# The last 512 tokens of a linear-attention layer as two groups of 256

## The reference

```python
xn = _ln(x, ln_w, ln_b)
q = xn @ Wq + bq
k = xn @ Wk + bk + (1.0 - src_mask) * -1000000.0
q = softmax(q.reshape(b, t, h, dh), axis=-1)
k = softmax(k.reshape(b, t, h, dh), axis=1)
v = ((xn @ Wv + bv) * src_mask).reshape(b, t, h, dh)
att = einsum('bnhd,bnhl->bhdl', k, v)
y = einsum('bnhd,bhdl->bnhl', q, att).reshape(b, t, d)
scale, shift = split(silu(emb) @ W_emb + b_emb, 2)
hh = _ln(y, ln2_w, ln2_b) * (1.0 + scale) + shift
return x + silu(hh) @ W_out + b_out
```

## Time and profile before

| what | value |
|---|---|
| median of 3 runs | 334.37 us (333.7 to 336.6) |
| the profiled execution, its own time | 336.49 us |
| its span, first to last instruction | 334.7 us |
| mean granted TensorE clock over the span | 0.985 of full speed |

### The profile page before, as it was taken

How to read it: one execution, slowest core, us unless ns; L and a number is a source line. 1 busy time by engine, 2 the same in 40 slices (tenths; PEclk the granted TensorE clock), 3 DMA queues, 4 the chain that set the end, 5 groups by cost and what they waited for, 6 DMA issues and landing times.

```text
span 334.7 us, 14404 instructions
## 1 busy us (share of the span) xinstructions
PE 315.3 (94%) x5644; PEld 269.0 (80%) x5644; DVE 277.3 (83%) x749; ACT 182.7 (55%) x360; POOL 198.3 (59%) x261
## 2 busy tenths in 40 slices
PE   3999999999999999999999999999999999998736
PEld 1478777988879898988888898989898888988625
DVE  3695888989898989989897979799898989886771
ACT  1327574566484755565574847565556648454240
POOL 2305137767766775767677667757676775747420
PEclk9999999999999999999999999999999999999896
DMA  7702010040404021030304040210304010101011
GB/s 238 256 0 66 20 47 4 2 129 2 127 5 118 7 66 59 11 115 0 125 0 125 0 125 0 71 55 25 101 0 125 0 63 0 66 4 63 4 66 63
DMA packets 19418, 19.68 MB, mean 59 GB/s; under 512 B 817, under 2 KB 18865, under 8 KB 19394
## 3 DMA queue, kind: packets, MB, share of 16 engines
q1 hardware_dynamic: 18144, 17.96, 17.2%
q10 hardware_dynamic: 1250, 1.39, 1.3%
HBM read 10.95 MB, written 8.39 MB: 58 GB/s over the span
## 4 chain that ended last, share of the span: by engine, by line
PE 87%; DVE 5%; POOL 3%; DMA 2%; issue 1%; ACT 1%; SPq 0%; POOLq 0%; DVEq 0%
PE bv L674 29%; PE bk L674 28%; PE by L674 13%; PE by L734 4%; PE by L745 4%; PE by L777 4%; PE by L724 4%; DMA q_t<-in_wv 2%; POOL y_s L350 1%; DVE ystat L647 1%; DVE y_s L640 1%; POOL yr L345 1%; DVE z_s L565 0%; DVE q_s L557 0%; DVE rq L636 0%
## 5 line engine op out<-in xcount | busy, mean ns | idle before, releaser
L408 ACT ACTIVATE k_t<-k_t 128x512 f32<-128x512 f32 x32 | 20.2, 632 | 55.9 <-DVE k_t L591 55.9
L243 POOL TENSOR_TENSOR h_lo<-h_s,h_hi 128x512 fp32r<-128x512 f32 x30 | 38.1, 1290 | 10.0 <-ACT h_hi L434 10.0
L239 POOL TENSOR_TENSOR z_s<-z_s,mod_shift 128x512 f32<-128x512 f32 x30 | 30.7, 1043 | 21.6 <-DVE z_s L565 21.6
L674 PE MATMUL bv<-w_o_hi,h_hi 128*128 128x256 f32 x128 | 35.1, 295 | 4.5 <-ACT h_hi L434 4.5
L358 POOL TENSOR_TENSOR x_all<-x_all,bo_all 128x1024 f32 (+1 forms) x16 | 38.3, 2396 | 0.0
L391 ACT ACTIVATE xt_hi<-by 128x512 fp32r<-128x512 f32 x32 | 17.5, 595 | 37.1 <-PE by L745 37.1
L587 DVE TENSOR_REDUCE kmax<-bk 128x8 f32<-128x512 f32 x32 | 22.0, 687 | 16.2 <-PE bk L674 16.2
L350 POOL TENSOR_SCALAR y_s<-y_s,yr 128x256 f32<-128x256 f32 x62 | 33.8, 558 | 2.6 <-POOL yr L347 2.2
L345 POOL TENSOR_TENSOR yr<-yr,neg_half 128x4 f32<-128x4 f32 x16 | 16.2, 1012 | 31.4 <-DVE yr L654 31.4
L674 PE MATMUL bv<-w_o_lo,h_hi 128*128 128x256 f32 x128 | 34.7, 292 | 0.0
L440 ACT ACTIVATE xhat<-x_all,xr 128x256 f32 (+1 forms) x64 | 33.1, 590 | 2.3 <-POOL xr L333 2.3
(11 more groups left out here) (106 smaller groups left out, 857.6 us busy)
## 6 DMA issues: line engine op xcount, KB each, us to landing
x_all<-in_x SPq DMA_DIRECT2D x16, 512.0 KB, 4.5
out<-x_all SPq DMA_DIRECT2D x15, 512.0 KB, 3.2
z_s<-in_w_emb ACTq DMA_DIRECT2D x1, 512.0 KB, 8.6
h_s<-in_w_emb ACTq DMA_DIRECT2D x1, 512.0 KB, 10.5
out<-x_all SPq DMA_DIRECT2D x2, 256.0 KB, 2.1
y_s<-in_wk SPq DMA_DIRECT2D x1, 256.0 KB, 3.3
q_t<-in_wq SPq DMA_DIRECT2D x1, 256.0 KB, 5.5
th<-in_cond_t ACTq DMA_DIRECT2D x1, 256.0 KB, 7.2
```

The costliest lines, as they stand in the source:

```text
L239: return eng.tensor_tensor(z, z, mod_shift[:, c, span(g, GB)].unsqueeze(2).broadcast_to([P, GB, SEQ]), ALU.add)
L243: return eng.tensor_tensor(h_lo[:, c, :], h_s[:, c, :], h_hi[:, c, :].bitcast(fp32), ALU.subtract)
L408: nc.scalar.activation(k_t[:, par, c, :], k_t[:, par, c, :], ACT.Exp).then_inc(kexp_d, 1)
L674: return nc.tensor.matmul(dst, lhsT, rhs, start=start, stop=stop)
```

## The change

The last 512 tokens become two groups of 256 tokens: 15 groups of four tiles and two of two, G = 17. There are 19 working turns where there were 18. The loop has five passes (turns 3 to 12), and turns 13 to 18 are unrolled. In groups 15 and 16 each operation over a group's tokens is half as wide, or there are half as many of them; the output product keeps its matmuls of 256 columns, 12 of them for such a group. Every semaphore count that was a multiple of the group number is now the sum of the tiles (`tile0`) or pairs of tiles (`pairs`) before the group. A group of two tiles has no qv tiles 2 and 3, so its turn goes from y to o at once. The first k of turn 16 waits for `ksub_d`, since no q tiles used its bank.

```diff
-    G = ROWS // GT
     T = GT // P
+    TILES = [4] * 15 + [2, 2]
+    G = len(TILES)
+    R = ROWS // GT
+    LOOP = 5
...
-            with eng.Fori(1, G // 2 - 1) as turn:
+            with eng.Fori(1, LOOP + 1) as turn:
                 body(2 * turn + 1, 1, True, True, True, True)
                 body(2 * turn + 2, 0, True, True, True, True)
-            for i in range(G - 1, G + 2):
+            for i in range(2 * LOOP + 3, G + 2):
                 at(i)
...
+        def tile0(g):
+
+            return sum(TILES[0:max(g, 0)]) if isinstance(g, int) else g * T
+
+        def pairs(g):
+
+            return tile0(g) // 2 if isinstance(g, int) else g * 2
+
+        def size(g):
+
+            return TILES[g] if isinstance(g, int) else T
...
+        def last_pair(g, e):
+
+            return pairs(g) + (min(e, size(g) // 2 - 1) if isinstance(g, int) else e) + 1
...
-                    for t in range(T) if not last_y(i) else (0, 1):
+                    for t in range(n // 2 if last_y(i) else n):
...
-                    for e in range(2):
-                        wait(act, ekt_d, 2 * g + e + 1)
+                    for e in range(size(g) // 2):
+                        wait(act, ekt_d, pairs(g) + e + 1)
...
-                    v_tile(i, par, 2)
-                    v_tile(i, par, 3)
+                    for t in range(2, size(i)):
+                        v_tile(i, par, t)
...
-                if F:
+                if F and size(i) > 2:
                     q_tiles(i, par, (2, 3))
...
-                        wait_apart(pe, qsub_d, 4 * i + c - 1)
+                        if not (isinstance(i, int) and i < 1):
+                            if size(i - 1) > 2:
+                                wait_apart(pe, qsub_d, tile0(i - 1) + c + 3)
+                            else:
+                                wait(pe, ksub_d, 2 * i + c - 1)
+                        n = size(i) * P
...
-                    qv_tile(i, 2)
-                    qv_tile(i, 3)
+                    for t in range(2, size(i)):
+                        qv_tile(i, t)
...
-                    for e in range(2):
-
-                        wait(pe, qsub_d, 4 * i + e + 1 if F else 4 * G)
+                    for e in range(size(g) // 2):
+
+                        wait(pe, qsub_d, tile0(i) + e + 1 if F else tile0(G))
```

More of the change, by code:

```diff
@@ L236, in shift, with h_low, cut, x_of @@
         def shift(eng, g, c):
-            z = z_s[:, c, :].rearrange("p (b s) -> p b s", s=SEQ)
-            return eng.tensor_tensor(z, z, mod_shift[:, c, span(g, GB)].unsqueeze(2).broadcast_to([P, GB, SEQ]),
+            n = size(g) * P
+            z = z_s[:, c, 0:n].rearrange("p (b s) -> p b s", s=SEQ)
+            return eng.tensor_tensor(z, z, mod_shift[:, c, batches(g)].unsqueeze(2).broadcast_to([P, n // SEQ, SEQ]),
                                      ALU.add)
[L242 to L253, removed]
+        def h_low(eng, g, c):
+            n = size(g) * P
+            return eng.tensor_tensor(h_lo[:, c, 0:n], h_s[:, c, 0:n], h_hi[:, c, 0:n].bitcast(fp32), ALU.subtract)
+        x_h = x.rearrange("(n p) d -> p n d", p=P)
+        o_h = out.rearrange("(n p) d -> p n d", p=P)
+        def tile0(g):
[4 more added lines that the diff above has]
+            return TILES[g] if isinstance(g, int) else T
+        def cut(first, n):
+            return slice(first, first + n) if isinstance(first, int) else bass.ds(first, n)
+        def x_of(g):
+            return x_all[:, cut(tile0(g), size(g)), :]
+        def x_tile(g, t):
+            return x_all[:, cut(tile0(g) + t, 1), :].rearrange("p n d -> p (n d)")
+        def batches(g):
+            return cut(tile0(g) * 2, size(g) * 2)
+        def last_pair(g, e):
+            return pairs(g) + (min(e, size(g) // 2 - 1) if isinstance(g, int) else e) + 1
         @block.sync
@@ L283, in _ @@
             steps(sp, body)
-            for e in range(2):
[L286 to L290, removed]
+            last = tile0(G - 1)
+            for e in range(size(G - 1) // 2):
+                sp.wait_ge(res_d, pairs(G - 1) + e + 1)
+                sp.dma_start(o_h[:, last + 2 * e:last + 2 * e + 2, :],
+                             x_all[:, last + 2 * e:last + 2 * e + 2, :]).then_inc(stored, 16)
+            sp.wait_ge(stored, 16 * (G - 1 + size(G - 1) // 2))
         @block.gpsimd
@@ L432, in body @@
                         wait(act, h_d, 2 * g + c + 1)
-                        wait(act, o_d, 2 * g)
-                        nc.scalar.activation(h_hi[:, c, :], h_s[:, c, :], ACT.Copy).then_inc(hhi_d, 1)
+                        wait(act, o_d, pairs(g))
+                        nc.scalar.activation(h_hi[:, c, 0:size(g) * P], h_s[:, c, 0:size(g) * P], ACT.Copy).then_inc(hhi_d, 1)
                 if N:
@@ L702, in qv_tile @@
                 if t < 2:
-                    wait(pe, qsub_d, 4 * i + t - 3)
-                    wait(pe, res_d, 2 * (i - 3) + t + 1)
+                    if not (isinstance(i, int) and i < 1):
+                        wait(pe, qsub_d, tile0(i - 1) + t + 1)
+                    if not (isinstance(i, int) and i < 3):
+                        wait(pe, res_d, last_pair(i - 3, t))
                 else:
@@ L719, in exp_k_transposed @@
                 wait(pe, kexp_d, 2 * g + 2)
-                for e in range(2):
-                    wait(pe, ys_d, 2 * (g - 1) + 2)
+                for e in range(size(g) // 2):
+                    wait(pe, ys_d, pairs(g))
                     for t in (2 * e, 2 * e + 1):
@@ L741, in body @@
                         if c == 0:
-                            wait(pe, xhat_d, 4 * i + 4)
-                        wait(pe, ys_d, 2 * (i - 2) + 2)
-                        for t in range(T):
+                            wait(pe, xhat_d, tile0(i + 1))
+                        if not (isinstance(i, int) and i < 2):
+                            wait(pe, ys_d, pairs(i - 1))
+                        for t in range(size(i)):
                             last = nc.tensor.transpose(bt[c][:, t * P:t * P + P], xhat[:, par, t, c * P:c * P + P],
@@ L782, in body @@
                     g = i - 1
[L783 removed]
+                    wait(pe, ek_d, pairs(g + 1))
                     wait(pe, zs_d, 2 * g)
[L785 to L786 removed]
+                    wait_apart(pe, v_d, tile0(g + 1))
+                    for b in range(2 * size(g)):
                         t, e = b // 2, b % 2
```

205 lines of the change are left out of this document (103 added, 102 removed).

## The result

The changed kernel takes 340.07 us (median of 4 runs, 338.24 to 340.90); before, beside it, 335.19. The ratio is 1.013, with a 95% interval of 1.0096 to 1.0165: slower by 1.3%, about 4.4 us. The forecast was 336.6 in a range of 333.4 to 339.2, with "within 1%" at 0.74 and "slower" at 0.20. It was wrong. The ratios compare only executions in the faster of two states and are not exactly the quotient of the two medians; where a change in us stands behind a ratio, it is worked out from the ratio.

What follows compares the result with a forecast made beforehand. TensorE bounds the full turns, a serial chain through all engines the last 30 us. Drain -12.2, earlier T -2.1, new turn +14.9, clock +1.6: +2.2 on the median 334.37 gives 336.6 us, range 333.4 to 339.2.

Steps and rivals of the forecast that it cites:

- Up to turn 15: nothing: Turns before 15: unrolling turns 13 and 14 costs 0, hidden by TensorE's work.
- plus and minus 0.8 us for pauses: Allowance for TensorE pauses like the known 0.79 us one: -0.8 to +0.8 us.
- Turn 15 and turn 16: Turn 15's T comes 2.1 us earlier; the new turn 16 adds 14.9 us between the two T.
- The wait for h_lo: In turns 15 and 16, o issues four matmuls, then waits for h_lo; 1.6 us in turn 15.
- T: Landmark: the moment at which the second qv tile of a turn is done.
- The drain: Serial chain behind the last T: shrinks from 37.0 to 24.8 us.
- clock term: Loss from TensorE's low clock on the path: 1.6 us, ends 0 and 4.5 us.
- Clock, one stretch of 1.6 us in o of turn 16: In o of turn 16, behind waits, one stretch at 1.2 GHz adds 1.6 us, all on the path.
- upper widths listed: Upper uncertainties: narrow ScalarE pieces +0.4, kv +0.3, pauses +0.8, clock +2.9 us.
- Rival 2: Turns 15 to 17: TensorE becomes short bursts at 1.2 GHz; +5.1, 339.5 us; chance 0.18.
- Rival 3: Waits of turns 15 and 16 don't come, GpSimd and VectorE being ahead; -2.5, 331.9 us; chance 0.12.
- Rival 1: Clock keeps its level over o of turn 16; +0.6, 335.0 us; chance 0.25.

Runs made afterwards that it cites:

- u1: Kernel before with 16 full groups, loop one pass shorter, so turns 13 and 14 are unrolled: 338.0 us, ratio 1.0062 to the kernel before.
- second series: The changed kernel run once more as it is, beside other runs on one chip: 342.9 us, ratio 1.0195 to the kernel before.
- r1: Changed kernel with its loop kept at six passes, so turns 13 and 14 stay in it: 338.19 us, ratio 1.0073 to the kernel before.
- rf1: Six-pass version of the changed kernel plus five unused TensorE matmuls in the h_lo waits of turns 15 and 16: 337.53 us, 1.0059 to the kernel before.

## Why the prediction was wrong

- **"Up to turn 15: nothing", unrolling at 0, plus and minus 0.8 us for pauses.** This step failed. It looked at turn 15, which was unrolled and had no gap, and took it for all unrolled turns. The one pause it knew (0.79 us) was already of this kind, as the packet 2.4 us ahead of it shows; the forecast gave it a few tenths more if a cover were gone. Unrolling two turns alone costs 2.1 us (u1), in the changed kernel's own trace 3.2 us with the low clock behind the pause, in its second series still more. Without this term the size holds: six passes gave +2.5 us, forecast +2.2.
- **Turn 15 and turn 16.** The wait for h_lo was right: 1.33 us, forecast 1.6. But o of turn 15 then ran at the low clock and ended 7.6 us behind T in r1, forecast 6.0. Taking the start of y for T, the two T lie 15.7 us apart in r1 (294.16 to 309.82), forecast 14.9. With the clock held up by fillers, yT waited 0.82 us for the normalized y and came 9.2 us behind T, much as forecast (1.1 and 9.0).
- **The drain.** Behind the second T r1 has 25.6 us (309.82 to 335.4), forecast 24.8 without the clock term. From the start of turn 15 to the end of the span r1 took 50.6 us (284.80 to 335.4), the kernel before 48.2. The forecast, without its clock term, has 48.8, with it 50.4.
- **Clock, one stretch of 1.6 us in o of turn 16.** The place was wrong: o of turn 16 stayed at 2.4 GHz, and the stretch fell in o of turn 15, where yT's wait hid more than half of it (rf1). So about 0.6 us of the term were spent there, and the rest stood in for 0.8 us by which the drain and 0.4 by which turn 15 were sized too short. That six passes come within 0.3 us of the forecast is partly luck.
- **Range and base.** The upper widths listed add to +4.4 us, 341.0; the range stopped at 339.2. The forecast stands on 334.37 us for the kernel before, which measured 335.19 beside the changed one; 0.8 us of the distance come from that.
- **Rivals.** Rival 2 forecast 339.5 us through clock losses above 2.7 us. The time came near it, by another mechanism for nearly half of it: u1 lost its 2.1 us with the clock at 1.00 behind the pauses. Rival 3 fell: o never found h_lo ready in turns 15 and 16. Rival 1 fell too, though its own claim, that o of turn 16 keeps its clock, came true: the clock fell in o of turn 15 instead.
- **What stayed open.** What sets the moment at which a packet of instructions starts, and with it why the pause comes in some unrolled turns and not in others, and why it doubled between two series of the same program.

## What to carry to other kernels

Splitting the last group shortens the drain only by the parts that scale with width, and adds a turn that pays the full latency of the group ahead of it. With six passes the new turn cost 15.7 us, while the shorter turn 15 and drain gave back 13.3 (1.7 and 11.5); the forecast had 14.9 against 14.3. Ask for the cost of unrolling separately: a dense run of small matmuls in code executed once can starve TensorE, and one gap put down to issue in the unrolled part of the old trace is a warning; look for an instruction packet ahead of it. Where TensorE idles before the last products, filler matmuls into a free bank were worth 2.3 to 2.7 us, more than all reordering tried here. Look at the granted clock behind them: nine of them with 1.87 us of idling behind did not keep it up, though no run changed their number alone.

## What the runs showed of the hardware

- In code executed for the first time TensorE can stand still for 1.5 to 2.3 us, nearly always among products issued about every 10 ns; TensorE's own unrolled code suffices. It goes on 2.2 to 2.75 us behind the start of an instruction packet. The Trainium skill, page "Runtime: NRT & Kernel Launch", section "Instruction fetch mechanics", says that the sequencer fetches 16 KiB blocks ahead and that crossing one is mostly hidden. The packets agree with the blocks (16384 bytes each); for this dense stretch the cost was not hidden, and the measurement decides.
- The granted clock fell behind waits of 1.3 us with y products before them (o of turn 15, in the changed kernel and in r1) and not behind like waits at another time (o of turn 16). Five filler matmuls, 1.2 us, in the wait kept it at 1.00; 14 in a wait of 4.45 us brought the last o from 5.50 to 3.34 us; nine, with 1.87 us of idling behind them, did not keep it up (20 matmuls in 4.17 us).
- VectorE's h_s of 256 columns took 780 and 956 ns beside GpSimd's work on SBUF and 0.44 us without it.
